# Layer 2's attention weights turned by DMA instead of TensorE, a compact layer 1, SyncE's transfers as an ordered list, and new orders for all engines

## The chip, the cores and the metric
One Trainium2 chip, one core of it. The metric is the device time of one launch in microseconds (us). The kernel has one core only, so the slowest core is that core.

## What is computed
128 graphs of 64 nodes with 256 features pass through four graph layers. After each one stands a residual and a layer norm. `mm3` below is how every product is done: both operands are split in a high and a low f16 part and three products are summed.

```python
# layer 0 (twice): out = D^-1 H B^-1 H^T (x W^T) + b, with relu and layer norm between, H = (adj != 0)
# layer 1:  agg = adj @ (x Wk);  w = 1/16 * rowsum(q * agg);  softmax over the 64 nodes;  w * v
# layer 2:  8 heads of 32;  scores = q k^T * scale * (adj + adj);  attn = softmax(scores);  attn @ v, Wo
# layer 3:  gate = sigmoid(rowsum(adj) * Wd + bd);  xg = x * gate;  QK = sigmoid(xg Wqk^T + bqk)
#           scores = QK QK^T / 16 * adj, divided by their row sum;  relu(attn @ xg Wl^T + bl + xg Wr^T)
x = _layernorm(x + _L0_gnn_ref(...)); x = _layernorm(x + _L1_gnn_ref(...))
x = _layernorm(x + _L2_gnn_ref(...)); x = _layernorm(x + _L3_gnn_ref(...))
```

## The kernel before
A group is four graphs: 256 nodes as two tiles of 128 partitions, each tile two graphs. There are 32 groups. The work on one group is cut into six streams (0 and 1: layer 0 and the start of layer 1; 2: the end of layer 1 and layer 2's q; 3: layer 2's k, v, scores and exp; 4: context, output product, gate; 5: layer 3). In step s, stream k works on group s - k, so a step holds all six streams on six different groups, and a group takes six steps. Steps 0 to 5 fill the pipeline (HEAD lists), steps 6 to 31 are full and run from a loop (ORDER lists), steps 32 to 36 drain it (TAIL lists).

Each stream is a Python generator per engine. It ends a piece at each `yield`. An order list names, piece by piece, which stream gives the engine its next piece; stream 6 is the set-up of the weights. So every engine's instruction stream is written out by hand and is executed in that order; engines wait for each other on semaphores that count. `at.n()`, `at.tile(t)`, `at.chain(...)` and `at.dma(...)` are the values to wait for, and a negative distance means an earlier group, for a buffer that is to come free.

TensorE has 35 pieces in a step. Those named later: stream 1 gives the first-layer output product, the second convolution, the turn of x1, `u` (`project_fm(bC, Gm, ...)`) and `uxT` (L661 on: `u` times x1, 12 products of 128 columns, of which only the two 64x64 diagonal blocks per tile are used later). Between `u` and `uxT` ScalarE casts the high part (`uh`) and VectorE the low part (`ul`), and `uxT` waits for `u_lo`. Stream 2 gives w_turned, w_back, w_sum, v1, the turn of x2, and q. Stream 3 gives k, v, two pieces of scores and two of `E` turned (L730, 4 f32 turns each). Stream 4 gives two pieces of context (`ctx`, L743), the turn of the context, the output product and the turn of xg. Stream 5 gives qk3, y3, s3 (L781, 64-column products), the turn of the attention (L787), o2 and o1.

After the exp of the scores (`E`, f32, ScalarE), TensorE turns it into a bank, ScalarE casts the high part `PTh` out of the bank, VectorE the low part `PTl`, and `ctx` multiplies both by `Vbd`.

SyncE issues all transfers, in the order of `step` (L455 on). q and k go to DRAM (`park`) and come back by head (`fetch`), v goes from `vst` to `Vbd` by four transfers (`place_v`). x is loaded twice (`xin`, `xres`), rows of adjacency three times (`aC` in blocks with zeros beside them, `acD`, `acG`), its transpose for layer 0 (`atA`) and for layer 3 (`atG`), the mask twice (`mrow`, `mcol`).

Of the kernel before, what the change touches and what calls it, by code (L numbers as in the profile page):

```python
# [29 lines left out]
P = 128  # L30
# [26 lines left out]
TAIL_POOL = [[1, 3, 1, 1, 1, 1, 1, 4, 5, 3, 2, 2, 4, 4, 3, 4, 5, 5, 5], [3, 4, 5, 2, 2, 3, 4, 4, 3, 4, 5, 5, 5], [3, 4, 5, 4, 4, 3, 4, 3, 5, 5, 5], [5, 4, 4, 4, 4, 5, 5, 5], [5, 5, 5, 5]]
# [7 lines left out]
def build(nc, x, adj, adj_t, mask, mask_col, w1t, b1, gamma, beta, w2t, b2, wqk1t, wv1, wqt, bq, wkt, bk, wvt, bv,  # L65
          wot, bo, wqk3t, bqk, wlt, bl, wrt, wd, bd, out):
    ctx = ExitStack()
    with ctx:
# [91 lines left out]
        xres = sb("xres", [P, 2, TILES, D])  # L160
# [34 lines left out]
        wscr = sb("wscr", [P, TOK])  # L195
# [3 lines left out]
        wrm = sb("wrm", [TILES, 2, NODES])  # L199
# [17 lines left out]
        PTh = sb("PTh", [P, TILES, 4, P], F16)  # L217
        PTl = sb("PTl", [P, TILES, 4, P], F16)
# [6 lines left out]
        acG = sb("acG", [P, 2, TILES, NODES])  # L225
        deg = sb("deg", [P, TILES])
# [22 lines left out]
        class At:  # L249
# [37 lines left out]
        def run(eng, order, head, tail, streams, set_up):  # L287
# [41 lines left out]
        def _(sp):  # L329
# [12 lines left out]
            mr = mask.rearrange("(g o k) -> g o k", o=1, k=TOK)  # L342
# [13 lines left out]
            def load_residual(at):  # L356
                if at.earlier(2):
                    sp.wait_ge(ev("preB"), at.n(-2)).then_inc(ev("sp_held"), 1)
                sp.dma_start(xres[:, at.par], at_group(xv, at)).then_inc(ev(f"xres_in{at.par}"), 16)

            def load_layer1(at):
                if at.earlier(2):
                    sp.wait_ge(ev("adj_masked"), at.n(-2)).then_inc(ev("sp_held"), 1)
                    sp.wait_ge(ev("w_masked"), at.n(-2)).then_inc(ev("sp_held"), 1)
                blocks(aC, adj, at, "C_in")
                sp.dma_start(mrow[:, at.par], mr[bass.ds(at.group(), 1)].rearrange("g o k -> (g o) k")
                             .broadcast_to([P, TOK])).then_inc(ev(f"C_in{at.par}"), 16)
# [21 lines left out]

            loads = [load_conv, load_residual, None, load_layer2, load_gate, load_layer3]  # L390
# [30 lines left out]

            def place_v(at):
# [27 lines left out]
            sp.wait_ge(ev("const"), 2)  # L450
# [6 lines left out]
            sp.wait_ge(ev("const"), 6)  # L457
# [1061 lines left out]
```

## Time and profile before

| | |
|---|---|
| median of 3 runs | 970.98 us (969.42 to 976.12) |
| profiled execution's own time | 970.12 us |
| its span, first to last instruction | 968.3 us |
| TensorE busy | 897.9 us, 93% of the span |
| VectorE busy | 788.5 us, 81% |
| ScalarE busy | 673.2 us, 70% |
| GpSimd busy | 664.9 us, 69% |
| DMA | 95.26 MB, mean 98 GB/s |
| mean granted TensorE clock | 0.981 |

A matmul in the profile lasts from its start to the modelled end of its pipeline, so neighbours overlap: what one costs TensorE is the distance from its start to the next one's start. The same holds, less strongly, for VectorE and ScalarE.

### The profile page before, as it was taken

Reading aid. Unit: us, or ns where it says so; the run is one execution under the profiler, and the core shown is the slowest. Engines: PE = TensorE matmul, PEld = TensorE weight load, DVE = VectorE, ACT = ScalarE, POOL = GpSimd, SP = SyncE. Lnnn points to the kernel's source line nnn. Section 1 sums busy time; section 2 is a strip of 40 time slices with the busy share of each in tenths; the row PEclk is TensorE's granted clock in tenths of the full one; section 3 lists DMA queues with packets and bytes.
Section 4 is the critical chain, followed back from the end, with each engine's and each line's share of the span. In section 5 each row is a group of like instructions: output and inputs, shape, how many; then the busy total and the mean of one; then the engine's idle time right before and its main releaser. Section 6 shows DMA issues by size and latency. Waiting matters only on the chain.

```text
span 968.3 us, 33947 instructions
## 1 busy us (share of the span) xinstructions
PE 897.9 (93%) x11996; PEld 782.4 (81%) x11996; DVE 788.5 (81%) x2548; ACT 673.2 (70%) x1484; POOL 664.9 (69%) x1005
## 2 busy tenths in 40 slices
PE   3677899999999999999999999999999999999873
PEld 2456678888988888888888888888898888887752
DVE  4667767889888888888888888888898888888772
ACT  2434577787777777787777777778777777776652
POOL 2646566777777777777777777777777777775431
PEclk9988999999999999999999999999999999999997
DMA  8203332444433333334433333333443333332420
GB/s 227 53 10 93 98 90 52 118 109 117 117 103 111 89 99 96 103 101 117 117 111 109 100 91 97 105 99 105 117 117 111 104 100 90 96 99 58 116 69 22
DMA packets 149006, 95.26 MB, mean 98 GB/s; under 512 B 59107, under 2 KB 148709, under 8 KB 148965
## 3 DMA queue, kind: packets, MB, share of 16 engines
q1 hardware_dynamic: 148964, 94.73, 35.2%
q8 instruction: 24, 0.39, 0.2%
q14 instruction: 18, 0.14, 0.0%
HBM read 60.86 MB, written 25.17 MB: 89 GB/s over the span
## 4 chain that ended last, share of the span: by engine, by line
PE 82%; DVE 7%; ACT 3%; POOL 3%; issue 2%; DMA 2%; SPq 1%; ACTq 0%; POOLq 0%; DVEq 0%
PE bank L520 20%; PE bank L522 19%; PE bank L521 19%; PE bank L545 6%; PE bank L730 3%; PE bank L743 3%; PE bank L805 2%; PE bank L719 2%; PE bank L633 2%; PE bank L781 1%; PE bank L794 1%; DMA Ks<-k_by_head 1%; PE bank L629 1%; PE bank L631 1%; PE bank L602 1%
## 5 line engine op out<-in xcount | busy, mean ns | idle before, releaser
L1358 POOL TENSOR_TENSOR rFl<-r,rFh 128x512 f16<-128x512 f32 x64 | 74.1, 1161 | 27.7 <-ACT rFh L816 27.7
L520 PE MATMUL bank<-z1h,W 128*128 128x256 f16 x256 | 72.5, 283 | 2.1 <-DVE z1l L1004 2.0
L521 PE MATMUL bank<-z1l,W 128*128 128x256 f16 x256 | 72.2, 282 | 0.0
L522 PE MATMUL bank<-z1h,W 128*128 128x256 f16 x256 | 72.0, 281 | 0.0
L1454 POOL TENSOR_TENSOR late<-late,Smx 128x512 f32<-128x512 f32 x64 | 66.7, 1044 | 4.9 <-DVE Smx L1261 4.8
L522 PE MATMUL bank<-W,rFl 128*128 128x256 f16 x256 | 70.0, 274 | 0.0
L520 PE MATMUL bank<-W,rFh 128*128 128x256 f16 x256 | 70.0, 274 | 0.0
L521 PE MATMUL bank<-W,rFh 128*128 128x256 f16 x256 | 70.0, 273 | 0.0
L1468 POOL TENSOR_TENSOR late<-g,late 128x512 f32<-128x512 f32 x32 | 40.7, 1271 | 34.2 <-ACT late L838 34.2
L869 ACT ACTIVATE r<-bank,b1c 128x256 f32<-128x256 f32 x128 | 53.0, 471 | 11.8 <-PE bank L522 11.8
L1358 POOL TENSOR_TENSOR xl<-xin,xh 128x512 f16<-128x512 f32 x32 | 37.6, 1174 | 25.6 <-ACT xh L816 25.5
L840 ACT ACTIVATE late<-preG,nbG,rsG 128x256 f32<-128x256 f32 x64 | 34.9, 592 | 27.9 <-POOL nbG L1375 27.8
L840 ACT ACTIVATE x<-preB,nbB,rsB 128x256 f32<-128x256 f32 x64 | 34.9, 593 | 24.6 <-POOL nbB L1375 24.5
L816 ACT ACTIVATE xgFh<-bank 128x512 f16<-128x512 f32 x32 | 19.1, 598 | 46.3 <-PE bank L545 46.3
L1004 DVE SCALAR_TENSOR_TENSOR x2Fl<-bank,x2Fh 128x512 f16<-128x512 f32 x32 | 22.1, 691 | 32.6 <-ACT x2Fh L816 32.6
L1380 POOL TENSOR_TENSOR gp<-late,bdb 128x512 f32<-128x512 f32 x32 | 40.6, 1268 | 10.4 <-ACT late L955 10.4
L816 ACT ACTIVATE y0h<-y 128x512 f16<-128x512 f32 x32 | 20.2, 630 | 38.1 <-DVE y L1173 38.1
L1010 DVE SCALAR_TENSOR_TENSOR qst<-bank,bqc,qst 128x256 f16<-128x256 f32 x64 | 28.0, 479 | 21.8 <-ACT qst L918 21.7
L545 PE MATMUL bank<-ident,late 128*128 128x128 f32 x256 | 41.7, 285 | 3.7 <-POOL late L1468 2.5
L520 PE MATMUL bank<-Wv,x2Fh 128*128 128x128 f16 x256 | 44.5, 219 | 0.0
L1261 DVE TENSOR_REDUCE Smx<-late 128x8 f32<-128x512 f32 x64 | 43.6, 682 | 1.1
L521 PE MATMUL bank<-Wv,x2Fh 128*128 128x128 f16 x256 | 44.5, 219 | 0.0
(285 smaller groups left out, 4302.4 us busy)
## 6 DMA issues: line engine op xcount, KB each, us to landing
Qs<-q_by_head SPq DMA_DIRECT2D x96, 128.0 KB, 2.5
Ks<-k_by_head SPq DMA_DIRECT2D x96, 128.0 KB, 2.5
Vbd<-vst SPq DMA_DIRECT2D x128, 66.0 KB, 2.1
xin<-x SPq DMA_DIRECT2D x32, 256.0 KB, 2.8
xres<-x SPq DMA_DIRECT2D x32, 256.0 KB, 2.9
q_by_head<-qst SPq DMA_DIRECT2D x32, 256.0 KB, 2.2
k_by_head<-kst SPq DMA_DIRECT2D x32, 256.0 KB, 2.2
out<-late SPq DMA_DIRECT2D x32, 256.0 KB, 2.6
```

The costliest lines, as they stand in the source:

```text
L520: pe.matmul(o, sh, mh, start=start, stop=False, skip_group_check=True)
L521: pe.matmul(o, sh, ml, start=False, stop=False, skip_group_check=True)
L522: return pe.matmul(o, sl, mh, start=False, stop=stop, skip_group_check=True)
L545: m = pe.transpose(o[:, c * TOK + t * P:c * TOK + (t + 1) * P], src[:, t, c * P:(c + 1) * P], ident_[:])
L816: return act.activation(dst, src, ACT.Copy, scale=scale)
L840: m = act.activation(dst[:, t], pre[k][:, t], ACT.Identity, bias=nb[k][:, t:t + 1], scale=rs[k][:, t:t + 1])
L869: m = act.activation(r[:, 2 * i + c], (bA, bB)[i][:, c * TOK:(c + 1) * TOK], ACT.Relu, bias=b1c[:, 2 * i + c:2 * i + c + 1], scale=1.0 / WS)
L1261: dve.tensor_reduce(Smx[:, t], Sm[:, t], AX.X, ALU.max).then_inc(ev("s_max"), 1)
L1358: return pool.tensor_tensor(dst, a, b, ALU.subtract)
L1380: return pool.tensor_tensor(dst, src, b[:].rearrange("p (o d) -> p o d", o=1).broadcast_to([P, TILES, D]), ALU.add)
L1454: pool.tensor_tensor(Ssb[:, t], Sm[:, t], Smx[:, t:t + 1].rearrange("p t h -> p h t").broadcast_to([P, HEADS, NODES]), ALU.subtract).then_ ...
L1468: pool.tensor_tensor(xg[:], g2[:], x3[:, at.par], ALU.mult).then_inc(ev("xg"), 1)
```

## The change
- **Layer 2's weights.** TensorE's two pieces that turn `E`, and the two casts out of the bank, are gone. ScalarE casts `E` (SBUF) to f16 in `Ehl[:, t, 0]`, VectorE subtracts it from `E` into `Ehl[:, t, 1]`, and SyncE turns both with one `dma_start_transpose` per tile (`turn_p`, 128 x 1024 f16) into `PT`. `ctx` waits for its completion.
- **Layer 1.** `aC`, `mrow`, `am`, `wscr` hold 64 columns in place of 128; `uxT` is 24 products of 64 columns into 64 partitions each, in place of 12 of 128; `adj_mask` brings rows of adjacency and mask in one transfer; `w_back` is a full 128-column turn.
- **Loads.** `xres` is gone: `xin` is kept until preB and gets the bias in place. `acG` is gone: `deg` is reduced from `acD`, in stream 3.
- **SyncE** runs from an order list too, 13 pieces in a step.
- **All order lists are new.** TensorE's now has 33 pieces.

```diff
-ORDER_PE = [3, 2, 3, 1, 0, 2, 4, 4, 5, 4, 2, 1, 0, 5, 0, 2, 5, 3, 3, 0, 1, 0, 5, 4, 1, 2, 3, 5, 5, 2, 3, 1, 0, 0, 4]
+ORDER_PE = [1, 2, 5, 3, 4, 4, 0, 2, 1, 2, 3, 0, 5, 0, 4, 2, 0, 0, 3, 1, 3, 5, 4, 1, 5, 2, 1, 5, 5, 0, 2, 4, 0]
+ORDER_SP = [3, 3, 3, 0, 0, 5, 3, 0, 3, 2, 4, 2, 2]
+ORDER_ACT = [1, 5, 3, 0, 2, 0, 0, 3, 5, 0, 4, 4, 5, 1, 0, 4, 0, 0, 1, 0, 2, 0, 0, 1, 5, 2, 3, 3, 4, 4, 3, 3, 2, 4, 5]
+ORDER_DVE = [0, 0, 0, 0, 1, 2, 0, 0, 2, 0, 0, 3, 0, 1, 4, 1, 2, 2, 4, 0, 4, 4, 1, 3, 0, 5, 2, 5, 2, 4, 2, 3, 3, 3, 5, 1, 5, 5, 3, 4, 4, 1, 4, 5, 2, 3, 1, 3, 5, 5, 0, 5, 0, 0, 3, 2, 4, 1]
+ORDER_POOL = [0, 1, 0, 0, 1, 0, 3, 1, 1, 1, 1, 4, 2, 2, 0, 3, 5, 0, 0, 4, 0, 4, 3, 4, 5, 5, 5, 0, 0]
...
+            def turn_p(at, t):
+                sp.wait_ge(ev("e_lo"), at.tile(t)).then_inc(ev("sp_held"), 1)
+                if at.earlier(1):
+                    sp.wait_ge(ev("ctx"), at.tile(t, -1)).then_inc(ev("sp_held"), 1)
+                sp.dma_start_transpose(PT[:, t].rearrange("p l c k -> p (l c) k"),
+                                       Ehl[:, t].rearrange("p l h k -> p (l h k)")).then_inc(ev(f"e_turned{t}"), 16)
...
-            sp.wait_ge(ev("const"), 2)
+            sp.wait_ge(ev("const"), 1)
+            load_x(At(0, None, 0))
...
-                    tok = slice(t * P, (t + 1) * P)
                     for k in range(2):
-                        m = mm3(bC[:, tok], uh[:, k, tok], ul[:, k, tok], x1Fh[at.par][:, k, tok],
-                                x1Fl[at.par][:, k, tok], k == 0, k == 1)
+                        for i, (uu, xx) in enumerate(((uh, x1Fh[at.par]), (uh, x1Fl[at.par]), (ul, x1Fh[at.par]))):
+                            for b in range(2):
+                                tok = slice(t * P + 64 * b, t * P + 64 * b + 64)
+                                m = pe.matmul(bC[64 * b:64 * b + 64, t * NODES:(t + 1) * NODES], uu[:, k, tok],
+                                              xx[:, k, tok], start=(k == 0 and i == 0), stop=(k == 1 and i == 2),
+                                              skip_group_check=True)
...
-                for t in range(TILES):
-                    pe.wait_ge(ev("exp"), at.tile(t))
-                    o = (bF0, bF1)[t]
-                    for hp in range(4):
-                        m = pe.transpose(o[:, hp * P:(hp + 1) * P],
-                                         E[:, t, 2 * hp:2 * hp + 2].rearrange("p h k -> p (h k)"), ident[:])
-                    m.then_inc(ev("e_turned"), 1)
-                    yield
...
+                    pe.wait_ge(ev(f"e_turned{t}"), at.chain(16, 16))
...
-                for t in range(TILES):
-                    act.wait_ge(ev("e_turned"), at.tile(t))
-                    cast(PTh[:, t].rearrange("p c k -> p (c k)"), (bF0, bF1)[t][:]).then_inc(ev("pt_hi"), 1)
+                    act.wait_ge(ev("exp"), at.tile(t))
+                    if at.earlier(1):
+                        act.wait_ge(ev(f"e_turned{t}"), at.chain(16, 16, -1))
+                    cast(Ehl[:, t, 0], E[:, t]).then_inc(ev("e_hi"), 1)
                     yield
...
-            dve.memset(aC[:], 0.0).then_inc(ev("const"), 1)
...
-                    dve.wait_ge(ev("pt_hi"), at.tile(t))
-                    low(PTl[:, t].rearrange("p c k -> p (c k)"), (bF0, bF1)[t][:],
-                        PTh[:, t].rearrange("p c k -> p (c k)")).then_inc(ev("pt_lo"), 1)
+                    dve.wait_ge(ev("e_hi"), at.tile(t))
+                    if at.earlier(1):
+                        dve.wait_ge(ev(f"e_turned{t}"), at.chain(16, 16, -1))
+                    dve.tensor_tensor(Ehl[:, t, 1], E[:, t], Ehl[:, t, 0], ALU.subtract).then_inc(ev("e_lo"), 1)
                     yield
```

## Rows read from the trace of the kernel before

**Rows 1.** Busy time by stage; columns: stretch, length, busy us (x instructions), clock, DMA.
```profile
120.00:200.00 80.00, 75.88 (x1031) 66.24 (x1032) 63.89 (x210) 57.44 (x126) 57.53 (x86) 1.00 0.33 91
200.00:800.00 600.00, 600.00 (x8337) 533.25 (x8336) 525.57 (x1731) 459.25 (x1024) 455.46 (x689) 1.00 0.38 106
...
860.00:920.00 60.00, 54.83 (x745) 46.01 (x743) 47.68 (x142) 39.52 (x86) 34.49 (x51) 0.97 0.29 82
```

**Rows 2.** Timeline of VectorE, two successive steps; columns: start us, us, what.
```profile
418.02 0.68 DVE L1179 SCALAR_TENSOR_TENSOR preB<-xres,bank 128x512 f32<-128x512 f32 x1
...
445.02 0.68 DVE L1179 SCALAR_TENSOR_TENSOR preB<-xres,bank 128x512 f32<-128x512 f32 x1
```

**Rows 3.** Timeline of TensorE in one steady step.
```profile
399.73 0.27 PE L520 MATMUL bank<-x1Fh,Gm 128*128 128x256 f16 x1
...
401.04 0.60 PE L545 MATMUL bank<-ident,x 128*128 128x128 f32 x4
401.48 0.60 PE L730 MATMUL bank<-ident,E 128*128 128x128 f32 x4
401.98 0.39 PE L794 MATMUL bank<-blr,ones 128*128 128x512 f16 x1
...
405.70 0.60 PE L730 MATMUL bank<-ident,E 128*128 128x128 f32 x4
406.14 0.22 PE L520 MATMUL bank<-x1Fh,uh 128*128 128x128 f16 x1
...
406.81 0.17 PE L629 MATMUL bank<-ones,rFh 128*128 128x1 f16 x1
```

**Rows 4.** Timeline of TensorE, same step, 64-column products and small turns.
```profile
410.80 0.27 PE L670 MATMUL bank<-ident,wpad 128*128 128x128 f32 x1
410.91 0.22 PE L520 MATMUL bank<-Wv,x2Fh 128*128 128x128 f16 x1
...
421.01 0.27 PE L522 MATMUL bank<-Wv,x1Fl 128*128 128x256 f16 x1
421.21 0.22 PE L781 MATMUL bank<-Qh 128*64 128x64 f16 x2
...
421.61 0.67 PE L719 MATMUL bank<-Ks,Qs 96*64 96x64 f16 x32
```

**Rows 5.** Timelines of TensorE, ScalarE and VectorE where nothing else was queued.
```profile
76.05 0.27 PE L522 MATMUL bank<-x1Fh,Gm 128*128 128x256 f16 x1
77.74 0.23 PE L520 MATMUL bank<-x1Fh,uh 128*128 128x128 f16 x1 [1.42 <-DVE ul L1004]
...
76.36 0.60 ACT L816 ACTIVATE uh<-bank 128x512 f16<-128x512 f32 x1 [0.28 <-PE bank L522]
...
76.99 0.69 DVE L1004 SCALAR_TENSOR_TENSOR ul<-bank,uh 128x512 f16<-128x512 f32 x1 [2.21 <-ACT uh L816]
```

**Rows 6.** A group of VectorE; columns: x count | busy us, mean ns | idle before.
```profile
L1302 DVE SCALAR_TENSOR_TENSOR Ql<-qt,Qh 128x512 f16<-128x512 f32 x32 | 21.6, 676 | 3.3 <-ACT Qh L984 3.3
```

**Rows 7.** DMA issues: count, KB each, median us from issue to landing.
```profile
q_by_head<-qst SPq DMA_DIRECT2D x32, 256.0 KB, 2.2
```

**Rows 8.** The x loads by tile: issue time, then longest way to landing.
```profile
L350 SPq DMA_DIRECT2D xin<-x x32: 378/399/469, 2.0 to 819.6; - x32
...
DMA to landing us min/median/max: 2.6/2.8/6.7
```

**Rows 9.** Groups of GpSimd with the columns of rows 6.
```profile
L1358 POOL TENSOR_TENSOR rFl<-r,rFh 128x512 f16<-128x512 f32 x64 | 74.1, 1161 | 27.7 <-ACT rFh L816 27.7
L1454 POOL TENSOR_TENSOR late<-late,Smx 128x512 f32<-128x512 f32 x64 | 66.7, 1044 | 4.9 <-DVE Smx L1261 4.8
L1408 POOL TENSOR_TENSOR rsq<-rsq 128x512 f32<-128x512 f32 x32 | 40.7, 1272 | 0.3 <-ACT rsq L877 0.3
L1468 POOL TENSOR_TENSOR late<-g,late 128x512 f32<-128x512 f32 x32 | 40.7, 1271 | 34.2 <-ACT late L838 34.2
```

**Rows 10.** Timeline of VectorE at the start.
```profile
1.45 0.48 DVE L1016 MEMSET aC<- 128x512 f32 x1
```

More of the change, by code:

```diff
@@ L274, in dma, with after @@
                 return self.j * (16 * per) + 16 * per * k if self.j is not None else 16 * per * k
+            def after(self):
+                return At(0, self.j, self.fixed + 1)
             def before(self):
@@ L285, in earlier, with run @@
                 return self.j is not None or self.fixed >= d
-        def run(eng, order, head, tail, streams, set_up):
+        def run(eng, order, head, tail, streams, set_up, early=0):
             pieces = set_up()
@@ L304, in run @@
             assert next(pieces, "end") == "end"
-            with eng.Fori(first // 2, last // 2) as j:
+            with eng.Fori(first // 2, (last - early) // 2) as j:
                 for par in range(2):
                     step(j, par, 0, LAST_LAG, order)
+            for s in range(last - early, last):
+                step(None, s, 0, LAST_LAG, order)
             for s in range(last, STEPS):
@@ L497, in _, with set_up, stream0 @@
-            first = LAST_LAG + 1
-            last = first + (GROUPS - first) // 2 * 2 - 2
-            for s in range(first):
-                step(None, s)
-            with sp.Fori(first // 2, last // 2) as j:
-                for par in range(2):
-                    step(j, par)
-            for s in range(last, STEPS + 1):
-                step(None, s)
+            def set_up():
+                return
+                yield
+            def stream0(at):
+                nxt = at.after()
+                more = at.j is not None or nxt.fixed < GROUPS
+                if more:
+                    load_x(nxt)
+                yield
+                if more:
+                    load_conv(nxt)
+                yield
+                if at.j is not None or at.fixed > 0:
+                    load_layer1(at)
+                yield
@@ new lines, in stream1, with stream2, stream3 @@
+            def stream1(at):
+                return
+                yield
+            def stream2(at):
+                park_q(at)
+                yield
+                fetch_q(at)
+                yield
+                load_layer2(at)
+                yield
+            def stream3(at):
+                park_k(at)
+                yield
+                fetch_k(at)
+                yield
+                place_v(at)
+                yield
+                for t in range(TILES):
+                    turn_p(at, t)
+                    yield
```

168 lines of the change are left out of this document (66 added, 102 removed).

## The prediction, made before the changed kernel was run

> **What bounds the kernel now.** I read the busy time by stage first. From 200 to 800 us TensorE is busy 600.00 us of 600 at full clock (2.4 GHz, granted 1.00), and from 120 to 200 us 75.88 of 80 [rows 1]. VectorE is busy 525.57 us of the same 600, ScalarE 459.25, GpSimd 455.46. TensorE never waits there, so the time is TensorE's work, and an edit is worth what it takes from that or what gap it opens. The timeline of VectorE gives the period: the same instruction of two successive steps starts at 418.02 and 445.02, 27.00 us per step [rows 2]. VectorE works 525.57/600 * 27.00 = 23.65 us of a step.
>
> The profile's duration of a matmul overlaps the next one's, so I read TensorE's costs as distances between starts. `u` takes 401.04 - 399.73 = 1.31 us [rows 3]; every product of twelve 256-column matmuls costs that.
>
> **The change part by part, for a full step.**
>
> *E is no longer turned on TensorE.* The two pieces take 401.98 - 401.48 = 0.50 and 406.14 - 405.70 = 0.44 us [rows 3]: -0.94.
>
> *uxT compact.* It takes 406.81 - 406.14 = 0.67 [rows 3]. The new form is that of s3, 24 products of 64 columns with 64 by 64 results: 421.61 - 421.21 = 0.40, and its entry costs 421.21 - 421.01 - 0.11 = 0.09 more than a plain successor [rows 4]. So 0.49 for 0.67: -0.18. `w_back` becomes a full turn of 0.11 [rows 4], about what its small form with its entry takes: 0.
>
> *Scores split.* The old order had both pieces of scores together, the new one puts the turn of x1 between: one more such entry, +0.1.
>
> TensorE's work: 27.00 - 0.94 - 0.18 + 0.1 = 25.98, so 26.0 us a step.
>
> *The gap that the new order opens.* This is the part that I weigh most. In the new ORDER_PE the pieces of stream 1 stand at indices 0, 8, 19, 23 and 26. `u` is 23, `uxT` is 26, and between them stand only the turn of the attention (stream 5, 0.11 like the small turn [rows 4]) and the turn of x2 (stream 2, 401.48 - 401.04 = 0.44 [rows 3]): 0.55 us. But `uxT` waits for `u_lo`, and the way there is a cast on ScalarE and a subtraction on VectorE. At 76 us the trace shows this chain alone: `u`'s last matmul starts at 76.05, its successor could start 0.11 later, `uh` starts at 76.36, `ul` at 76.99, and `uxT` at 77.74 [rows 5]. 77.74 - 76.16 = 1.58 us. TensorE must stand still for 1.58 - 0.55 = 1.03 us in every full step. The old order had six other pieces there and no gap (600.00 of 600). ScalarE has other pieces queued until about `u`'s end, which may add up to 0.1; I take 1.05.
>
> 25.98 + 1.05 = 27.03 us a step.
>
> *The other engines.* VectorE's `e_lo` reads SBUF in place of a bank: like Ql, 0.68 [rows 6], what the old one cost. `deg` moves, `wscr` halves (below 0.1). 23.6 of 27.0 us, so VectorE doesn't bound. GpSimd has, between the cast of the rectified half and the gated x that TensorE turns, two rFl (1.16), two shifts (1.04), rsq (1.27) and xg (1.27) in a row [rows 9], 2.32 + 2.08 + 2.54 = 6.94 us, with smaller pieces among them; placed on TensorE's pieces by hand it ends about when the turn of xg is due. I take 0.1 us a step for it, bounds 0 and 0.5. So 27.13.
>
> *The turn by DMA.* No row shows a DMA that turns. In the new order VectorE makes `e_lo` of tile 1 as its piece 54 of 58, an estimated 0.7 us after the end of TensorE's `q` (the pieces before it wait for the row sums just ahead of q). `ctx` of tile 1 follows after xg's turn (0.44), four products of the size of `u` (stream 0's last piece, stream 1's first, qk3, k; 4 * 1.31 = 5.24), a small turn (0.11) and the first ctx (24 small products like s3's, 0.40): 6.19 - 0.7 = 5.5 us to cover issue, transfer and completion (tile 0: over 8). The nearest rows: 256 KB of f16 out of SBUF land 2.2 us after the issue [rows 7] and the issue takes 0.40 [rows 8], so 2.6; the slowest 256 KB load landed after 6.7 [rows 8], so 7.1. By the lower row it is hidden, by the upper ctx is 1.6 us late. It is nearest to the first (same bytes, SBUF side), with more for its small blocks: I take 4.5 and 0 on the path. Behind the two turns on SP stand q's park and fetch and layer 3's load; the scores that need q come over half a step later.
>
> The Trainium skill speaks for this: "DMA: Bandwidth & Descriptors", section on latency and other measured facts, gives an effective 261 GB/s for such a turn, by which 256 KB take 1.0 us beside the fixed part. But "VectorE: DVE Perf Modes", section on the three transpose paths, gives 1309 ns for one 128x128 block by DMA; eight in a row would be an estimated 10.5 us, 5.0 beyond the cover, and the sum would be 5.0 us a step higher. Nothing here shows which holds.
>
> *The loads* that go (xres, acG, two blocks, mask column) were hidden: worth 0; without cover 0.4 us of SP's issue each [rows 8].
>
> **The sum.** Steps 6 to 31 are 26 full ones: 26 * (27.13 - 27.00) = +3.4. Start: the first load of adjacency no longer waits for the memset of `aC`, -0.5 [rows 10]. Steps 3 to 5 (TensorE busy 75.88 of 80 us) keep part of the 0.94: -2. The other filling steps have new orders: 0, bounds -8 and +8. Draining (54.83 of 60 us busy, then less [rows 1]): -1 for work gone, +2 for the last group's way through the DMA (0.6 + 0.7 + 3 to 4.5 in place of 0.4 + 0.6 + 0.7, partly beside the other streams). Together +1.9 on 970.1, the profiled execution's own time (span 968.3): 972.0. The median of the three runs is 0.9 above that execution, so I forecast 973.
>
> **The rivals.**
>
> *A. Forecast*: gap of 1.05 at uxT eats what was taken off; turn hidden. 973; its own range 958 to 984 (the GpSimd bound 0.4 * 26 = 10 upward, the filling steps and 0.2 us a step in the reading downward).
>
> *B. ctx waits for the turn* (the other side). It decides from 5.5 us on. Each us beyond is a us a step over about 28 steps. At 7.1 us it costs 1.6 * 28 = +45: 1018. Middle 0.8 late: 995. For it: no row has such a transfer, and it comes at the end of VectorE's step. Against: 2.2 us landings of the same bytes.
>
> *B2. The blocks are turned one after another.* Then a turn takes 8 times something. With half of the 2.2 us landing for each it is 8.8 us, 3.3 late: 973 + 3.3 * 28 = 1065. This is the mechanism of the Trainium skill's 1309 ns above; by that figure it would be an estimated 973 + 5.0 * 28 = 1113.
>
> *C. The gap isn't there*, since `ul` comes sooner than the chain at 76 us says, or other pieces absorb it: -1.05 * 26 = -27: 946. Against it: neither engine can start before `u` ends, and both durations are constant in the trace.
>
> *D. VectorE or GpSimd loses more in the new order*, 0.5 to 0.8 us a step: 985 to 993. For it: 23.6 of 27 us are taken and every wait of VectorE for TensorE is lost time.
>
> **How the numbers follow.** A 0.50, B 0.23, B2 0.07, C 0.10, D 0.10. The number is A's. Left out below 952: most of C (0.09). Left out above 1016: B2 and the end of B (0.10). A measurement of this kernel can tell about 1%, 961 to 981, from no change. Faster: C and 0.04 of A, 0.14. Slower: B2 0.07, B 0.22, D 0.09, A 0.03, 0.41. Same: the rest, 0.45.
>
> **What would show it.** The period (preB to preB) 27.1, not below 26.8. In the full steps TensorE idle once a step before `uxT`, about 1.0 us, released by `ul`; its busy time falls from 600 to about 577 in 600. The two turn pieces gone and s3's form in `uxT`. No wait of TensorE at the first ctx products for the DMA that writes PT; its landing under 5. If PT's landing is above 5.5 and ctx waits, B or B2 holds. If the gap before `uxT` is much under 1.0, C holds. Wrong too, if a wait that I don't name costs over 0.3 us a step.

## The result: 1002.2 us, 3.2% slower

The changed kernel takes 1002.17 us (median of 4 runs, 999.77 to 1004.09), the kernel before 970.20 beside it. The ratio is 1.032, 95% interval 1.0288 to 1.0352. The forecast was 973 in 952 to 1016, with 0.41 for slower: the range holds, the number and the likeliest case do not. The profiled execution, the longest of the four, has a span of 1002.2 us against 968.3, so 33.9 us are to be found.

Busy time by stretch of the changed kernel, columns as in [rows 1]. The third line begins at the preG of the last full step, the fourth is the filling (to group 6's preB):

```profile
120.00:200.00 80.00, 68.40 (x902) 57.51 (x903) 61.47 (x184) 50.08 (x111) 48.08 (x71) 0.94 0.36 85
200.00:800.00 600.00, 580.07 (x8368) 506.42 (x8368) 548.77 (x1731) 467.48 (x1020) 471.86 (x689) 1.00 0.42 109
882.00:1002.20 120.20, 82.67 (x1016) 62.41 (x1013) 68.21 (x197) 53.55 (x113) 42.81 (x69) 0.87 0.33 77
34.00:215.80 181.80, 143.10 (x1702) 117.48 (x1703) 122.25 (x380) 100.90 (x219) 105.99 (x153) 0.88 0.30 70
```

The same two end stretches of the kernel before:

```profile
863.50:968.30 104.80, 78.10 (x1044) 62.72 (x1042) 69.18 (x203) 54.48 (x115) 44.20 (x70) 0.92 0.24 68
34.00:202.00 168.00, 140.48 (x1678) 118.34 (x1679) 119.98 (x382) 100.87 (x223) 106.15 (x153) 0.94 0.28 76
```

In the full steps TensorE is now idle 20 us of 600, which is what the forecast meant. The loss is at the ends: draining takes 120.2 in place of 104.8 us. TensorE is busy 4.6 us longer there (82.67 for 78.10) with fewer instructions, at a granted clock of 0.87 in place of 0.92, and idle 10.8 us longer. VectorE's timeline dates it: group 6's preB, then two successive steps of preB as in [rows 2], then the preG of the last full step:

```profile
215.76 0.67 DVE L1184 SCALAR_TENSOR_TENSOR preB<-xin,bank 128x512 f32<-128x512 f32 x1
...
432.30 0.67 DVE L1184 SCALAR_TENSOR_TENSOR preB<-xin,bank 128x512 f32<-128x512 f32 x1
...
459.39 0.66 DVE L1184 SCALAR_TENSOR_TENSOR preB<-xin,bank 128x512 f32<-128x512 f32 x1
...
882.04 0.69 DVE L1336 SCALAR_TENSOR_TENSOR preG<-bank,late 128x512 f32<-128x512 f32 x1 [0.66 <-PE bank L811]
```

In the kernel before the two end marks are these:

```profile
202.04 0.68 DVE L1179 SCALAR_TENSOR_TENSOR preB<-xres,bank 128x512 f32<-128x512 f32 x1
...
863.50 0.69 DVE L1330 SCALAR_TENSOR_TENSOR preG<-bank,late 128x512 f32<-128x512 f32 x1 [0.37 <-PE bank L805]
```

The full step is 27.09 us here and 27.04 in the next (mean 27.07; 27.00 in [rows 2]): +1.7 over 24 steps. Group 6's preB comes 13.7 us later (215.76 - 202.04), draining takes 15.4 longer. The remaining 3.1 is that preG stands 3.1 us later in a step of the new order. 13.7 + 1.7 + 3.1 + 15.4 = 33.9.

The gap of the full step, on TensorE's timeline, where [rows 3] had none, with the small turn, the turn of x2, and the wait:

```profile
444.31 0.27 PE L794 MATMUL bank<-ident,SAs 128*128 128x128 f32 x1
444.42 0.60 PE L558 MATMUL bank<-ident,x 128*128 128x128 f32 x4
445.88 0.22 PE L678 MATMUL bank<-x1Fh,uh 128*64 128x64 f16 x2 [0.87 <-DVE ul L1010]
...
446.38 0.39 PE L801 MATMUL bank<-blr,ones 128*128 128x512 f16 x1
```

TensorE's waits from 200 to 800 us have one row (total, times, longest; L678 is uxT). Below it is what the tile PT says of the turn by DMA (duration of the issue, first and last start; time from the issue's start to landing; who waited over the whole run; L750 is ctx):

```profile
PE bank L678 <- DVE ul L1010: 19.9, 23, 0.9
```

```profile
L422 SPq DMA_TRANSPOSE PT<-Ehl x64: 1231/1269/1939, 107.6 to 958.2; - x64
...
  PE bank L750: 5.4, 6
...
DMA to landing us min/median/max: 3.1/3.1/5.1
```

So in the full steps the turn is hidden. The low part of tile 1 on VectorE, its turn on SyncE and ctx of both tiles on TensorE, in one full step:

```profile
451.01 0.69 DVE L1275 TENSOR_TENSOR Ehl<-E,Ehl 128x512 f16<-128x512 f32 x1
...
452.38 1.26 SPq L422 DMA_TRANSPOSE PT<-Ehl  x1
...
456.84 0.95 PE L750 MATMUL bank<-Vbd,PT 128*64 128x66 f16 x48
```

The low part ends at 451.70, and ctx of tile 1 is the second half of the last row, so it starts at about 457.3: a cover of 5.6 us, of which 0.7 pass before the issue and 3.1 until the landing. All waits for PT are outside the full steps. From 34 to 217 us, the filling, they are these; the rest of the 5.4 is in draining:

```profile
PE bank L750 <- DMA PT<-Ehl: 0.8, 2, 0.5
```

### The profile page after: what moved, and what is told of

Same layout as the page of the kernel before. It is cut to its first block, busy times and chain, and to the rows that moved or that the text cites. A ratio compares the mean times of both kernels' runs of the same rounds, so it can differ in the third digit from the quotient of the medians.

```text
span 1002.2 us, 34399 instructions
## 1 busy us (share of the span) xinstructions
PE 887.3 (89%) x12124; PEld 755.9 (75%) x12124; DVE 817.3 (82%) x2548; ACT 684.6 (68%) x1484; POOL 682.3 (68%) x1005
## 4 chain that ended last, share of the span: by engine, by line
PE 71%; DVE 16%; ACT 4%; DMA 3%; issue 3%; POOL 2%; SPq 1%; DVEq 0%; ACTq 0%; POOLq 0%
PE bank L533 17%; PE bank L535 16%; PE bank L534 16%; PE bank L558 4%; PE bank L750 3%; PE bank L811 2%; PE bank L734 2%; DVE stF L1111 2%; DVE preF L1295 2%; DVE ul L1010 2%; DVE late L1264 2%; DMA PT<-Ehl 2%; PE bank L678 2%; PE bank L646 1%; PE bank L788 1%
## 5 line engine op out<-in xcount | busy, mean ns | idle before, releaser
L533 PE MATMUL bank<-W,rFh 128*128 128x256 f16 x256 | 71.7, 280 | 1.4 <-DVE W L1010 1.4
L534 PE MATMUL bank<-W,rFh 128*128 128x256 f16 x256 | 71.7, 280 | 0.0
L1371 POOL TENSOR_SCALAR veB<-mvB 128x2 f32<-128x2 f32 x32 | 6.1, 192 | 69.3 <-DVE mvB L1116 69.3
L859 ACT ACTIVATE Pf<-bank,Dinv 128x128 f32<-128x128 f32 x64 | 20.0, 364 | 45.7 <-DVE Dinv L1152 45.7
L1275 DVE TENSOR_TENSOR Ehl<-E,Ehl 128x512 f16<-128x512 f32 x64 | 46.2, 722 | 1.1 <-ACT Ehl L822 1.1
L558 PE MATMUL bank<-ident,x 128*128 128x128 f32 x256 | 41.0, 284 | 6.4 <-ACT x L844 3.3
L1010 DVE SCALAR_TENSOR_TENSOR HBl<-HT,be,HBh 128x128 f16<-128x128 f16 x64 | 45.0, 745 | 1.0
L534 PE MATMUL bank<-Wv,x2Fh 128*128 128x128 f16 x256 | 45.6, 222 | 0.0
L533 PE MATMUL bank<-Wv,x2Fh 128*128 128x128 f16 x256 | 45.6, 222 | 0.0
L535 PE MATMUL bank<-Wv,x2Fl 128*128 128x128 f16 x256 | 45.5, 222 | 0.0
L1364 POOL TENSOR_TENSOR y0l<-y,y0h 128x512 f16<-128x512 f32 x32 | 37.5, 1171 | 10.9 <-ACT y0h L822 9.2
```

The costliest lines, as they stand in the source:

```text
L533: pe.matmul(o, sh, mh, start=start, stop=False, skip_group_check=True)
L534: pe.matmul(o, sh, ml, start=False, stop=False, skip_group_check=True)
L535: return pe.matmul(o, sl, mh, start=False, stop=stop, skip_group_check=True)
L558: m = pe.transpose(o[:, c * TOK + t * P:c * TOK + (t + 1) * P], src[:, t, c * P:(c + 1) * P], ident_[:])
L1010: return dve.scalar_tensor_tensor(out=dst, in0=src, scalar=scale, in1=hi, op0=ALU.mult, op1=ALU.subtract)
L1275: dve.tensor_tensor(Ehl[:, t, 1], E[:, t], Ehl[:, t, 0], ALU.subtract).then_inc(ev("e_lo"), 1)
```

## The experiments

Each ran beside the kernel before. "Filling" is the time of group 6's preB, "draining" the time from the last full step's preG to the end, both of one profiled execution. In the changed kernel they are 215.8 and 120.2, before 202.0 and 104.8. Executions of one kernel differ by some us (the four of the changed kernel span 999.77 to 1004.09), so a difference of two such figures is good to a few us only.

**Is the gap worth anything?** The changed kernel, TensorE's list alone:

```diff
-ORDER_PE = [..., 1, 5, 2, 1, 5, 5, 0, 2, 4, 0]
+ORDER_PE = [..., 1, 5, 2, 5, 5, 1, 0, 2, 4, 0]
```

> The changed kernel with one edit: in the full steps' order of TensorE, uxT stands behind o2 and o1 in place of ahead of them. Theory (a gap of 0.9 us before uxT eats what was taken off TensorE; head and tail cost the other 32 us): the period falls from 27.07 to about 26.1 us, the gap vanishes, 26 steps * 0.95 = 25 us less, near 977 us; filling and draining steps as in the changed kernel. Rival (VectorE, busy 24.7 us of 27.07, is the real pace and the gap only shows it): the gap moves to another product, the period stays above 26.7, less than 10 us are won.

1050.31 us, ratio 1.084 (1.0772 to 1.0907). The theory fell. The rival is right that the gap moves and that the step stays above 26.7, but neither expected a loss of 48 us. The full step became 28.9 us. TensorE's waits from 300 to 700 us (L801 is o2, L604 a product of stream 0, L558 a turn, L686 the turn of w):

```profile
PE bank L801 <- DVE SAl L1010: 16.8, 14, 1.2
PE bank L604 <- DVE HBl L1010: 6.6, 13, 0.6
PE bank L558 <- DVE preG L1336: 4.6, 14, 0.3
PE bank L686 <- DVE wpad L1207: 2.2, 14, 0.2
```

o2 now waits for SAl, which VectorE's list still has behind ul, and VectorE's w_raw waits for uxT with preG queued behind it. One list changed alone turns one gap into four. So all three were changed:

```diff
-ORDER_PE  = [..., 1, 5, 2, 1, 5, 5, 0, 2, 4, 0]
+ORDER_PE  = [..., 1, 5, 2, 5, 1, 5, 0, 2, 4, 0]
-ORDER_ACT = [..., 0, 0, 1, 5, 2, 3, ...]
+ORDER_ACT = [..., 0, 0, 5, 1, 2, 3, ...]
-ORDER_DVE = [..., 3, 5, 1, 5, 5, 3, 4, 4, 1, 4, 5, 2, 3, 1, 3, 5, ...]
+ORDER_DVE = [..., 3, 5, 1, 5, 5, 3, 4, 4, 5, 4, 1, 2, 3, 3, 1, 5, ...]
```

> The changed kernel with o2 ahead of uxT on TensorE, as in the earlier run, but with the other two engines' full-step lists following: ScalarE casts SAh ahead of uh, VectorE does SAl and the second half of F's statistics ahead of ul, and El0 ahead of w_raw. My theory (the only loss of a full step is TensorE's wait for the chain u, uh, ul of 0.9 us; here a wait for SAl of some 0.4 to 0.5 us takes its place): full step 26.5 to 26.7 us, 24 steps of it 9 to 13 us off, time 989 to 994 us. Rival V (VectorE or GpSimd, busy 24.7 and more of 27.07 us, are as tight as TensorE, and a wait for one of them comes up elsewhere): full step 26.9 to 27.3 us, time 999 to 1006 us.

1000.89 us (ratio 1.029, 1.0242 to 1.0339), full step 27.17. My theory fell, rival V holds. TensorE's waits, 300 to 600 us:

```profile
PE bank L801 <- DVE SAl L1010: 4.6, 11, 0.4
PE bank L558 <- POOL late L1474: 3.7, 11, 0.4
```

The wait for SAl is the one expected (0.42 us a step), but a second, for GpSimd's gated x, takes nearly as much (0.34). The gap can be moved, and most of what comes off it comes up at the next engine. The gated x ends the 6.94 us run of GpSimd which the forecast had given 0.1.

**What does the turn by DMA cost?** It was left out, all lists kept. The casts into `Ehl`, which had waited for the turn of the earlier group, wait for its ctx:

```diff
-                sp.dma_start_transpose(PT[:, t]..., Ehl[:, t]...).then_inc(ev(f"e_turned{t}"), 16)
...
-                    pe.wait_ge(ev(f"e_turned{t}"), at.chain(16, 16))
+                    pe.wait_ge(ev("e_lo"), at.tile(t))
...
-                                              PT[:, t, pt, hp, 64 * b:64 * b + 64], Vbd[...]
+                                              Ehl[:, t, pt, 2 * hp + b], Vbd[...]
```

> The changed kernel without the transfer that turns E: the context product reads the unturned f16 parts (so the turn is left out of the computation), all lists as they are. Theory L (the new lists of the filling and draining steps are what costs the 32 us): period 27.07, filling and draining hardly faster, 0 to 8 us less in all. Theory T (the way of E over SyncE and DMA, 3 to 5 us long, is what costs there): filling and draining steps fall back to near their old length, 20 to 30 us less, near 975.

992.18 us (ratio 1.0208, 1.0159 to 1.0258), 10 less than the changed kernel. Full step 27.07, unchanged; filling 211.0, draining 114.8, so 4.8 less at the front and 5.4 at the back. But not all of the 4.8 is the turn's. Group 2's preB, in the changed kernel and then here, is already 3.4 us apart, and the first turn is issued at 107.6:

```profile
90.74 0.68 DVE L1184 SCALAR_TENSOR_TENSOR preB<-xin,bank 128x512 f32<-128x512 f32 x1
```

```profile
87.32 0.68 DVE L1180 SCALAR_TENSOR_TENSOR preB<-xin,bank 128x512 f32<-128x512 f32 x1
```

From 40 to 60 us the granted clock was 0.67 in the changed kernel's execution and 0.80 here. The run with the filled gap above, whose filling lists and turns are those of the changed kernel, had 0.82, its group 2's preB at 86.8 and group 6's at 211.4. So those 3.4 us are a slower start of the one execution. The turn's part in filling is 1.4 us (TensorE waits 0.8 for it), in draining 5.4 (waits of 4.5): about 7 us in the traces, at most 10 by the medians. The other 22 have other causes.

Is it SyncE's line, where a turn that waits for E holds up loads?

```diff
-HEAD_SP[3] = [3, 3, 0, 3, 3, 0, 0, 2, 3, 2, 2]
+HEAD_SP[3] = [3, 3, 0, 3, 0, 0, 3, 2, 2, 3, 2]
-TAIL_SP[0] = [3, 3, 4, 3, 3, 5, 2, 3, 2, 2];  TAIL_SP[1] = [3, 3, 5, 3, 4, 3, 2, 3, 2, 2]
+TAIL_SP[0] = [3, 3, 4, 3, 3, 5, 2, 2, 2, 3];  TAIL_SP[1] = [3, 3, 5, 3, 4, 3, 2, 2, 2, 3]
```

> The changed kernel with three of SyncE's lists rewritten: in step 3 the two turns stand behind the loads of the next group and the park and fetch of q, in the first two draining steps the second turn stands last. Nothing else changes. Theory Q (a turn that waits for E holds up what is queued behind it on SyncE, and that is most of the 10 us that the run without turns gained): step 3 gets 3 to 5 us shorter, draining 2 to 4 us, time 993 to 998 us. Rival (the 10 us are ctx waiting for the turn itself, which is now issued later still): time 1000 to 1010 us.

1007.55 us (ratio 1.0349, 1.0309 to 1.0389): the rival. Step 3, from group 2's preB to group 3's, is as long as it was (34.6 us). TensorE's largest wait while draining, of the changed kernel and then of this one:

```profile
PE bank L750 <- DMA PT<-Ehl: 4.5, 4, 2.2
```

```profile
PE bank L750 <- DMA PT<-Ehl: 9.9, 5, 4.6
```

So it is ctx that waits for the turn itself, the longer the later it is issued. With fewer groups under way there is less work between El and ctx than the cover of a full step.

**Is it the one load of x**, which must now wait for preB in SyncE's line? The second load was put back:

```diff
-                    sp.wait_ge(ev("preB"), at.n(-2)).then_inc(ev("sp_held"), 1)
+                    sp.wait_ge(ev("x_lo"), at.n(-2)).then_inc(ev("sp_held"), 1)
                 sp.dma_start(xin[:, at.par], at_group(xv, at)).then_inc(ev(f"x_in{at.par}"), 16)
...
+                load_residual(at)
                 if at.j is not None or at.fixed > 0:
                     load_layer1(at)
```

> The changed kernel with x loaded twice again: x for the cast waits only for the earlier group's x_lo, a second load into xres waits for preB and stands with layer 1's loads; all lists as changed. Theory X (load_x now waits in SyncE's line for preB of the group before last, and what stands behind it is late while the pipeline fills): filling is 3 us or more shorter (group 6's preB before 212.8), time 995 us or less. Theory L (the lists, not this load): filling and time as in the changed kernel within 2 us, 1000 to 1004, one DMA issue of 0.4 us a step on SyncE being hidden; the full step stays 27.07.

1001.16 us (ratio 1.0297, 1.0262 to 1.0333), full step 27.07: the same time as the changed kernel. The profiled execution is the fastest of the four (997.03; the others 1001.05 to 1001.63), with filling 213.0, 2.8 less where "within 2 us" was expected, and draining 115.8. By the median this part of the change costs nothing that can be told; a cost of some us at the ends isn't excluded.

**Compact layer 1 alone**, in the kernel before with its own lists:

```diff
+                        for i, (uu, xx) in enumerate(((uh, x1Fh[at.par]), (uh, x1Fl[at.par]), (ul, x1Fh[at.par]))):
+                            for b in range(2):
+                                tok = slice(t * P + 64 * b, t * P + 64 * b + 64)
+                                m = pe.matmul(bC[64 * b:64 * b + 64, t * NODES:(t + 1) * NODES], uu[:, k, tok], ...)
```

> The kernel before with the compact layer 1 alone (64-column uxT, one transfer for rows of adjacency and mask, half-size products with the mask), its lists untouched. My term: uxT 0.67 to 0.49 us, 0.18 a step: period 26.82, and 0.5 us at the start: 970 - 6 = about 964 us. Rival: the switch into and out of 64-column products costs as much as they save, 970.

969.96 us, ratio 0.9983 (0.9951 to 1.0014), full step 26.99 for 27.00. The saving didn't come. TensorE's timeline shows where half of it went: uxT takes 457.65 - 457.14 = 0.51, 0.16 less than before, but the turn of E ahead of it, 0.44 in [rows 3], now takes 457.14 - 456.62 = 0.52. The other 0.08 isn't in these rows.

```profile
456.62 0.60 PE L731 MATMUL bank<-ident,E 128*128 128x128 f32 x4
457.14 0.22 PE L663 MATMUL bank<-x1Fh,uh 128*64 128x64 f16 x2
...
457.65 0.18 PE L627 MATMUL bank<-ones,rFh 128*128 128x1 f16 x1
```

**Is it the new lists?** The changed kernel with the lists of before, translated piece by piece (E's turns dropped from TensorE's, the new casts inserted, SyncE's pieces in the old sequence):

```diff
-ORDER_PE = [1, 2, 5, 3, 4, 4, 0, 2, 1, ...]
+ORDER_PE = [3, 2, 3, 1, 0, 2, 4, 4, 5, ...]
-ORDER_SP = [3, 3, 3, 0, 0, 5, 3, 0, 3, 2, 4, 2, 2]
+ORDER_SP = [3, 3, 5, 3, 0, 0, 0, 2, 4, 3, 3, 2, 2]
```

> The changed kernel (turn by DMA, compact layer 1, one load of x and of degrees' adjacency) with the order lists of the kernel before, converted to the new pieces: TensorE's two turn pieces struck out, the low parts at their old places, SyncE's list k's park and fetch, store, v, x, adjacency, layer 1, q's park, layer 3's load, the two turns, q's fetch, layer 2's load. Theory L (lists): filling and draining as before or a little faster, and the full steps at TensorE's work, 27.00 - 0.94 - 0.18 = 25.9 us (the turn lands 3.1 us after its issue, ctx comes 4.4 us after e_lo): 970 - 28 + 0 to 5 = about 945 us. Theory T (the DMA leg): the filling and draining steps stay 20 to 30 us longer than before, 965 to 975 us, even if the period is 25.9.

1034.01 us (ratio 1.0639, 1.0592 to 1.0686), far off what was expected. The full step is 28.04, filling 214.4, draining 131.8, in which TensorE waits 17.3 us for PT. The same without the turn:

> The changed kernel with the lists of the kernel before, and without the turn of E by DMA: ctx reads the unturned weights, so the turn of the softmax weights is the part of the computation that is left out. It is the fourth corner of a square: new lists with the turn (1002), new lists without it (992), old lists with it (1034), and this. Theory L (outside the full steps the new lists themselves cost some 22 us): with the old lists and no turn to wait for, filling and draining are those of the kernel before within 4 us (group 6's preB at 198 to 206, from group 30's preB to the end 114 to 122), a full step takes 26.1 to 27.0 us (26.99 less the two turns of E on TensorE, 0.94, of which a gap elsewhere may take all), and the time is 945 to 972 us. Theory T (the pieces that the change takes off TensorE were what filled its waits at either end, whatever the list): filling stays 8 us or more longer, draining 10 us or more longer than in the kernel before, time 980 us or more.

1007.16 us (ratio 1.0347, 1.0308 to 1.0387). Neither theory holds whole: filling is 204.4, nearly that of before, as L has it; draining is 115.5, 10.7 longer than before, as T has it; and the full step is 28.04, which neither had. The chain of waits shows why:

```profile
549.81 0.90 ACT x L840 x2
550.71 0.53 ACT E L944
...
551.26 0.49 ACT Ehl L818
...
551.80 0.27 ACT SAh L818
...
552.09 0.30 DVE SAl L1006
...
552.43 0.39 PE bank L797
```

My translation had put the cast Ehl between E and SAh, ahead of o2. Moved to where the kernel before had its first cast, in the filling and draining lists too:

```diff
-ORDER_ACT = [..., 2, 3, 3, 5, 0, 0, 2, 1, 0, 4, 3, 2, ...]
+ORDER_ACT = [..., 2, 3, 5, 0, 0, 2, 1, 0, 4, 3, 3, 2, ...]
```

> The run with the old lists and no turn by DMA (1007 us; the turn of the softmax weights is the part left out), with one piece moved in ScalarE's lists. The kernel before has no cast of E's high part between E0 and SAh; my conversion of its lists had put it there, and the trace of that run shows a ring of waits through it (casts on ScalarE, E, Ehl, SAh, then SAl, o2, preG's end of the bank, x3, xg, xh, xl, y0l) that is 28.03 us long whatever TensorE has to do. Here the cast stands directly ahead of E1, where the kernel before had its first cast. Theory R (that piece is what stretched the full step, and filling and draining with it): full step 27.3 to 27.7 us, TensorE's wait for SAl 0.5 us shorter, draining from the last full preG 4 to 7 us shorter than 115.5, time 982 to 994 us. Stronger form of it: the rest of the gap goes too, full step 26.9 to 27.2, time 968 to 980. Rival: the ring has another tight link (one load of x, degrees' new place), full step 28.0, time 1003 us or more.

988.52 us (ratio 1.0164, 1.0132 to 1.0195), full step 27.48: theory R in time, in the step and in TensorE's wait for SAl (0.75 us a step before the move, 0.2 after). Draining got 1.8 us shorter, not 4 to 7. The stretches of filling and draining:

```profile
34.00:202.90 168.90, 138.15 (x1716) 113.88 (x1717) 121.03 (x380) 100.72 (x223) 105.51 (x152) 0.93 0.24 67
875.90:989.60 113.70, 82.79 (x1040) 63.65 (x1038) 70.24 (x202) 54.95 (x115) 45.13 (x70) 0.84 0.22 62
```

Against the run without the turn on the new lists (211.0, 27.07, 114.8): the new lists cost 8.0 us in filling, save 0.41 in each of 24 full steps, put preG 3.1 later in the step, and cost 1.1 in draining: 8.0 - 9.8 + 3.1 + 1.1 = 2.4, the difference of the two spans (992.0 and 989.6). Of the 8.0, 6.5 are step 3: 34.0 us (121.33 - 87.32) on the new lists, 27.5 (113.29 - 85.78) on the old. One part of it can be seen. In step 3 of both runs on new lists, with the turn and without, VectorE's pair of HBl takes 2.28 us, where it takes 0.60 in the kernel before, and TensorE waits 1.8 for it. These are the rows of VectorE, GpSimd and TensorE in the changed kernel:

```profile
120.86 2.28 DVE L1010 SCALAR_TENSOR_TENSOR HBl<-HT,be,HBh 128x128 f16<-128x128 f16 x2
...
120.56 1.16 POOL L1364 TENSOR_TENSOR xl<-xin,xh 128x512 f16<-128x512 f32 x1
121.68 1.31 POOL L1386 TENSOR_TENSOR gp<-late,bdb 128x512 f32<-128x512 f32 x1
...
123.20 0.23 PE L604 MATMUL bank<-HBh,HT 128*128 128x128 f16 x1 [1.80 <-DVE HBl L1010]
```

**Did E's turns hold TensorE's clock up?** E's two turns were put back, in the run with the old lists and no turn by DMA as it was before the cast was moved, as filler: ctx overwrites them unread. The next group's exp waits for them.

```diff
+                for t in range(TILES):
+                    pe.wait_ge(ev("exp"), at.tile(t))
+                    for hp in range(4):
+                        m = pe.transpose(o[:, hp * P:(hp + 1) * P], E[:, t, 2 * hp:2 * hp + 2]..., ident[:])
+                    m.then_inc(ev("e_pe"), 1)
+                    yield
```

> The earlier run with the old lists and no turn by DMA (1007 us), and the two turns of E put back on TensorE at their old places in its list, but as filler: ctx overwrites them unread, and reads the unturned weights (that part of the computation is left out, as before). Strictly more work than that run: 8 transposes, 0.94 us, a step, and a wait for the exponential ahead of each. Theory T (those pieces filled TensorE's waits for SAl, y0l and others in a full step and kept its clock up while the pipeline drains): full step 26.9 to 27.3 us instead of 28.04, last full preG to the end 103 to 109 us instead of 115.5, time 968 to 980 us, that is faster for more work. Rival O (more work is more time; what lengthened those steps is the new way of making the weights on ScalarE and VectorE, and the one load of x): full step 28.0 to 29.0 us, draining 114 us or more, time 1005 to 1030 us.

1004.12 us (1.0342, 1.0297 to 1.0388), full step 28.02, draining 111.3 at a clock of 0.90:

```profile
888.70:1000.00 111.30, 80.83 (x1068) 63.62 (x1066) 69.06 (x202) 54.69 (x115) 46.09 (x70) 0.90 0.22 63
```

Without the filler draining was 115.5 at 0.83:

```profile
891.50:1007.00 115.50, 83.38 (x1040) 63.69 (x1038) 70.21 (x202) 54.62 (x115) 45.70 (x70) 0.83 0.21 61
```

More instructions and less busy time, at a higher clock. But the full step didn't move, the 4.2 us are no more than two executions can differ by, and the intervals of the two times overlap. T isn't shown, and the draining is below O's range too. On the new lists, filler late in the step:

> The run with the new lists and no turn by DMA (992 us; the turn of the weights is the part left out), with the same filler on TensorE: in a full step the first behind o1 and the second behind q, in the other steps ahead of the last two pieces and at the end. Theory T: draining from the last full preG is 104 to 110 us instead of 114.7, filling up to 3 us shorter, the full step grows by the 0.94 us of work less what falls into the gap (27.9 to 28.1, as the filler stands behind the gap). So with 24 full steps 992 + 22 - 5 to 10: 1004 to 1009 us. Rival O: draining 114 to 118 us and filling unchanged or longer, time 1014 to 1020 us.

1027.68 us (1.0586, 1.0539 to 1.0633), full step 28.25 (+1.2 for 0.94 of work), draining 116.2: for O, though above its range. And the old lists with filler and the turn by DMA:

> The first of these three with the turn by DMA in it again, that is the whole changed computation on the old lists, with the turns of E kept on TensorE as filler. Against that run it prices the DMA leg alone (wait of ctx, SyncE's line, traffic). With new lists the leg cost 10 us, with old ones 27 us (1034 less 1007). Theory D (the cost is where the old list leaves less time from El to ctx than the leg takes, and in SyncE's line at both ends): 15 to 27 us more than the first of these three, with TensorE waits for PT in filling and draining. Rival: the old list gives the leg time once the filler restores its rhythm, 3 to 10 us more.

1034.19 us (1.0635, 1.0585 to 1.0686), 30 more than without the turn by DMA. D holds in its mechanism, 3 us above its range. TensorE's waits for PT, first while filling, then while draining:

```profile
PE bank L760 <- DMA PT<-Ehl: 7.4, 4, 3.9
```

```profile
PE bank L760 <- DMA PT<-Ehl: 17.1, 8, 5.5
```

The old lists leave less time between El and ctx. On them the turn by DMA costs 27 to 30 us, on the new ones 10 at most. The new lists make room for the DMA, and are slower in filling.

## Why the prediction was right in the range and wrong in the case

That the range holds is luck. It reached to 1016 for rival B, ctx waiting for the turn in every step, and that doesn't happen in a single full step. The case it was centred on, A with 958 to 984, has the full step right and misses the time by 29 us, all of it outside the full steps.

- *The full step*: 27.13 forecast, 27.07 measured. The gap before uxT is there, 0.87 to 0.9 for 1.05, released by ul. TensorE's work is 580.07/600 * 27.07 = 26.17 for 25.98. GpSimd's 0.1 did not show, but its case D lies just behind, as the filled gap showed.
- *uxT -0.18*: a term that failed. The piece did get shorter (0.50), but its neighbour grew by 0.08 in the compact run, whose step didn't change.
- *The turn*: 4.5 us taken, 3.1 measured, within the bounds 2.6 and 7.1; the cover is 5.6 for 5.5. Rivals B and B2 fail in the full steps. Of the two figures of the Trainium skill the one in "DMA: Bandwidth & Descriptors" fits (3.1 less the 1.27 of the issue leaves 1.8 for 256 KB with all that is fixed). The 1309 ns that "VectorE: DVE Perf Modes" gives for one block do not add up over eight, as the prediction's estimate had it: 10.5 against 3.1.
- *"0 on the path"*: the step that failed first. The cover of 5.5 us was counted in a full step and carried over to the ends. There it is shorter, and the DMA costs 1.4 + 5.4 = 6.8 us by the traces and up to 10 by the medians, where the sum had 0 in filling and "+2" in draining.
- *"The other filling steps have new orders: 0, bounds -8 and +8"*: measured +8.0, the upper bound; 6.5 of it is step 3. The "-2" of steps 3 to 5 didn't come either: TensorE is busy 68.40 of 80 us there, not 75.88.
- *Draining "-1 + 2"*: measured +15.4. The turn's way is 5.4, the lists 1.1, and 8.9 (113.7 - 104.8) come with neither; the sum had no term for them.

By place, from single executions: filling 13.7 = slower start 3.4, turn 1.4, lists 8.0, rest 0.9; draining 15.4 = turn 5.4, lists 1.1, rest 8.9. In that rest, the run with old lists, no turn and the cast moved against the kernel before, TensorE is busy 4.7 us longer (82.79 for 78.10, at a clock of 0.84 for 0.92) and idle 4.2 longer. Of the 4.2, a wait for y3l that grew by 2.4 us is the largest part; its rows in the kernel before and in that run (L781 and L784 are s3):

```profile
PE bank L781 <- DVE y3l L1004: 2.4, 2, 1.4
```

```profile
PE bank L784 <- DVE y3l L1006: 4.8, 3, 2.4
```

So the lower clock can account for some 4.7 of the 8.9 by TensorE's own work. With two levels, 1.2 and 2.4 GHz, a mean of 0.92 over 104.8 us is 0.08 * 2 * 104.8 = 16.8 us at the lower one; in the changed kernel it is 0.13 * 2 * 120.2 = 31, and with the old lists, no turn and the cast moved 0.16 * 2 * 113.7 = 36. Whether the missing turns of E let the clock fall, or whether longer waits elsewhere did, stays open: each row is one execution, and the filler's effect is not beyond the intervals. Not tried was work on TensorE placed in the draining steps alone.

## What to carry to other kernels

A transfer that is hidden in the full step of a pipeline has to be priced again for the steps that fill and drain it: there the work that covers it is missing. Here the turn cost nothing in 26 full steps and about 7 us in the 11 around them. The orders of those steps have to be priced too: one filling step of the new order took 6.5 us more. Work taken off the bounding engine is worth nothing where the order then waits for a chain through two other engines; look for the next wait behind the one that is removed. In orders written out by hand, change the lists of the other engines with the one that you change, and keep a new piece off the stretch between a cast and what the bounding engine waits for.

## What the runs showed of the hardware

- The issue of a DMA that turns takes 1.27 us on SyncE, three times the 0.40 of a plain one [rows 8].
- A VectorE instruction on 128x128 f16 took up to 1345 ns where it took 354 at most before. The tile HBl, before and then after the change:

```profile
L1004 DVE SCALAR_TENSOR_TENSOR HBl<-HT,be,HBh x64: 328/332/354, 10.1 to 844.9; 128x128 f16<-128x128 f16 x64
```

```profile
L1010 DVE SCALAR_TENSOR_TENSOR HBl<-HT,be,HBh x64: 338/352/1345, 8.8 to 862.3; 128x128 f16<-128x128 f16 x64
```

The timelines of VectorE and GpSimd in one full step show the pair of HBl (1.52 us for both) ending at 457.58, just after a GpSimd subtraction that began 0.2 us behind it and ends at 457.44:

```profile
456.06 1.52 DVE L1010 SCALAR_TENSOR_TENSOR HBl<-HT,be,HBh 128x128 f16<-128x128 f16 x2
...
456.26 1.18 POOL L1364 TENSOR_TENSOR y0l<-y,y0h 128x512 f16<-128x512 f32 x1
```

The Trainium skill, "SBUF — State Buffer", section "Who interferes with whom", says that a VectorE instruction with two inputs in SBUF and a GpSimd instruction that reads SBUF exclude each other; the trace agrees. It lengthens VectorE's busy time (548.77 for 525.57 of 600, part of it this). In the full steps no wait of TensorE comes of it; in step 3 of the filling, with two GpSimd instructions in a row beside the pair, it is the wait of 1.8 us shown above.
- With uxT as products of 64 columns in place of 128, the 128-column turn before it took 0.52 us in place of 0.44.
- Executions with the same instructions up to there differed in the granted clock from 40 to 60 us, 0.67 in the changed kernel's and 0.82 in that of the run with the filled gap, and in group 2's preB, 90.7 and 86.8 us.
